# Another order of each engine's calls within a step of the attention stage

## The chip, the cores and the metric

The kernel runs on one core of a Trainium2 chip. The metric is the device time of one execution in microseconds; the figure compared is the median over several runs. A separate execution is recorded by the profiler and gives the trace.

## The reference, cut to what matters

The kernel computes a block of three parts over an input of 2 sequences x 4096 tokens x 256 features: a routed feed-forward part (8 experts, each token goes to its best two), a linear-attention part, and a second routed feed-forward part. The change touches only the attention part. Its core is a scan over chunks of 64 tokens, per sequence and head:

```python
def step(S, ch):
    Q, K, V, bt = ch
    Kb = K * bt
    Vb = V * bt
    A = jnp.eye(C) + jnp.tril(jnp.einsum('bhcd,bhed->bhce', Kb, K), -1)
    T = solve_triangular(A, I, lower=True)
    W = T @ Kb
    U = T @ Vb
    St = S.swapaxes(-1, -2)
    mid = U - W @ St
    O = Q @ St + jnp.einsum('bhcd,bhed->bhce', Q, K) * M @ mid
    S_new = S + mid.swapaxes(-1, -2) @ K
    return (S_new, O)
...
x = x + 0.5 * _L0_ffn_ref(_layernorm(x), ...)
x = x + _L0_attn_ref(_layernorm(x), ...)
x = x + 0.5 * _L0_ffn_ref(_layernorm(x), ...)
```

Q, K and V come from three projections, a causal convolution over 4 tokens and a silu; Q and K are normed. The output is normed per head, projected and added to x. The kernel also works out, while attention still runs, the gate of the second feed-forward part (which experts each finished token goes to) and scatters the finished rows into lists of rows per expert.

## The kernel before, in words

`build` runs three stages one after the other with a barrier between them: `ffn1`, `attention`, `ffn2`. In `attention` a tile is 128 tokens of each of the two sequences; there are NS = 32 tiles. `steps_of` unrolls the stage into 35 steps and a few more for the last gates. One step works on several tiles at once, like a pipeline: each engine's `body(f, g, t, s, u, v)` gets

- `f`: the tile whose norm, projections, convolution, silu and turning back run now (the front);
- `g`: the tile one behind, whose Gram products run and whose 16x16 diagonal blocks are inverted on GpSimd (`spread_blocks`, `take_blocks`, `invert_blocks`, `collect_inverses`; the blocks go through memory outside the core and back by small transfers on SyncE's queue, which end in the tiles `r16` and `i16`);
- `t`: two behind, whose inverse is grown from 16 to 32 to 64 (`first_products16`, which reads `r16` and `i16`, to `second_products64`);
- `s`: three behind, whose recurrent state, output and residual run (`state_in`, `out_in`, `mids`, `outputs`, `state_out`, `out_turn`, `out_project`, `residual`, `store_result`);
- `u`: four behind, whose gate products run;
- `v`: a batch of four finished tiles (with a position 0 to 3 in the cycle of four steps), whose routing runs (`load_batch`, `gate_norm`, `gate_first` in position 1, `gate_second`, `gate_exps`, `gate_sums` in position 2, `gate_scores`, `gate_ends`, `gate_places` and three `gate_scatter` calls in position 3, five more in position 0 of the next cycle).

The steps are called by their position 0, 1, 2, 3 in the cycle of four here. In the first three steps only `f`, then `g`, then `t` are there; in the last ones `f`, then `g`, then `t` are missing.

Nothing schedules the work at run time: every engine executes its calls in the order in which its `body` names them, and waits on semaphores where an operand or a buffer is not ready. The five `body` functions are the order written out by hand. SyncE executes no arithmetic; its `body` is the order in which the transfers of its queue are issued, and a wait there holds all transfers behind it. Among the functions that the change moves:

- `load_batch` (SyncE): reads a batch of four finished tiles back, two transfers of 512 KB, for the scatters.
- `load_weights` (SyncE): reads the expert weights of the second feed-forward part, in the step of the last tile.
- `column_sums` (TensorE) and `column_sums_out` (VectorE): sums over the gate's weights, once, in the first step that has a `t`.
- `clear_buffers` (VectorE): twelve memsets, once, in the step of the first tile.
- `x_low` (VectorE): the low part of the turned input, without which the projections `qkv` don't start. `history`: the three last tokens before the convolution.
- `remainder` (VectorE): V minus what the state gives, between `state_in` and `mids`. `residual` (VectorE): x plus the projected output; `out_in` of the next step waits for it, since it writes the same bank `ob`.
- `raw_out`, `tap0`, `silus`, `gate_turned` (ScalarE): copies of the projections, first tap of the convolution, silus, copy of the turned gate input.

## Time and profile before

| | |
|---|---|
| time, median of 3 runs | 1627.17 us (1624.81 to 1630.52) |
| time of the profiled execution | 1628.22 us |
| its span, first to last instruction | 1626.5 us |
| mean granted TensorE clock | 0.909 of full speed |
| attention stage in the span | about 397 to 1366 us |
| busy in the span: TensorE, VectorE, ScalarE, GpSimd | 83%, 76%, 54%, 61% |
| a step in the middle of attention | 26.3 to 28.4 us |

The profiled execution took 1.05 us more than the median of the three runs. 1.72 us of it lie outside the span. The rows further down have the start in us from the start of the span, the length in us, the engine, the line and operation, what is written from what, and the count; in brackets stands the idle time of the engine before it and the instruction whose end released it.

### The profile page before, as it was taken

To read this page: it belongs to the slowest core of one execution; us is meant where nothing else is said; L and a number is where in the kernel's file an instruction comes from. 1 tells how busy PE (TensorE), PEld (TensorE's weight loads), DVE (VectorE), ACT (ScalarE), POOL (GpSimd) and SP (SyncE) were. 2 spreads that over 40 slices of the span, in tenths; PEclk is the share of its full clock that TensorE was granted. 3 is DMA by queue.
4 is the path that set the end of the run, shared out by engine and by line. 5 is a ranking of instruction groups with operands and counts; after the bars stand their busy time and mean duration, and the time that the engine had idled before them with its cause. 6 is when DMAs were issued, how large, how long until landed. Compare 5 with 4: busy or idle time off the path is not lost. (4 is left out here: it accounts for less than half of the span.)

```text
span 1626.5 us, 36945 instructions
## 1 busy us (share of the span) xinstructions
PE 1344.8 (83%) x11688; PEld 1250.9 (77%) x11688; DVE 1237.7 (76%) x3235; ACT 875.4 (54%) x1725; POOL 986.1 (61%) x1719
## 2 busy tenths in 40 slices
PE   7673994994679999999999999899999761995996
PEld 7673994994568888888888888788888751995896
DVE  6664772673679999999999999899999645673574
ACT  2123772771356666657566666565666412772773
POOL 4762673575356566676675866766767622475366
PEclk8555997997699999999999999999999975998898
DMA  6426976671011213122213231222222245885782
GB/s 208 154 102 173 311 257 226 224 251 61 10 30 38 57 37 78 38 76 62 68 40 77 63 75 39 75 65 61 53 73 61 68 120 149 260 273 185 250 273 95
DMA packets 224026, 195.90 MB, mean 120 GB/s; under 512 B 105556, under 2 KB 186714, under 8 KB 223840
## 3 DMA queue, kind: packets, MB, share of 16 engines
q1 hardware_dynamic: 190560, 117.21, 26.4%
q0 software_dynamic: 24576, 67.94, 11.5%
q10 hardware_dynamic: 8704, 8.39, 1.8%
q8 instruction: 102, 1.67, 0.5%
q14 instruction: 84, 0.69, 0.1%
HBM read 103.68 MB, written 96.10 MB: 123 GB/s over the span
## 5 line engine op out<-in xcount | busy, mean ns | idle before, releaser
L1563 DVE SCALAR_TENSOR_TENSOR raw_w<-attn_raw,taps,raw_w 128x256 f32<-128x256 f32 x576 | 252.0, 495 | 17.9 <-ACT raw_w L1971 16.3
L468 PE MATMUL ffn_both<-ws,ffn_xhi 128*128 x1152 | 203.9, 289 | 0.6 <-issue 0.2
L2225 POOL TENSOR_TENSOR attn_inv<-attn_inv,attn_term 64x14 f32<-64x14 f32 (+6 forms) x448 | 147.8, 330 | 35.1
L468 PEld LDWEIGHTS ffn_both<-ws,ffn_xhi 128*128 128x128 f32 x1152 | 164.3, 192 | 3.0 <-issue 3.0
L2222 POOL TENSOR_TENSOR attn_term<-attn_small,attn_inv 64x14 f32<-64x14 f32 (+6 forms) x448 | 139.0, 310 | 35.1
L457 PE MATMUL ffn_both<-ident,ffn_xb 128*128 128x128 f32 x576 | 82.0, 290 | 93.7 <-ACT ffn_xb L752 93.7
L1202 PE MATMUL attn_fr<-attn_xhi,wqkv 128*128 128x256 f32 x768 | 148.7, 296 | 8.4 <-ACT attn_bth L1978 6.8
L457 PEld LDWEIGHTS ffn_both<-ident,ffn_xb 128*128 128x128 f32 x576 | 70.1, 150 | 95.9 <-ACT ffn_xb L752 74.9
L491 PE MATMUL ffn_yb<-ws,ffn_hhi 128*128 x576 | 119.5, 292 | 6.2 <-DVE ffn_hlo L667 6.2
L1202 PEld LDWEIGHTS attn_fr<-attn_xhi,wqkv 128*128 128x128 f32 x768 | 113.6, 194 | 10.0 <-ACT attn_bth L1978 7.4
L662 DVE TENSOR_TENSOR ffn_hid<-ffn_both,ffn_sil 128x512 f32<-128x512 f32 x72 | 49.8, 692 | 88.2 <-ACT ffn_sil L764 88.2
L468 PE MATMUL ffn_both<-ws,ffn_xlo 128*128 x576 | 116.1, 283 | 0.0
L657 DVE TENSOR_TENSOR ffn_xlo<-ffn_both,ffn_xhi 128x1024 fp32r<-128x1024 f32 x72 | 87.8, 1219 | 36.9 <-ACT ffn_xhi L759 36.8
L829 POOL DMA_INDIRECT second_rows<-ffn_more_rows,ffn_to x64 | 63.1, 985 | 85.3 <-DVE ffn_to L652 69.3
L752 ACT ACTIVATE ffn_xb<-ffn_more_rows 128x256 f32<-128x256 f32 x120 | 62.1, 591 | 78.3 <-DMA ffn_more_rows<-first_rows 42.5
L491 PEld LDWEIGHTS ffn_yb<-ws,ffn_hhi 128*128 128x128 f32 x576 | 94.2, 191 | 7.2 <-issue 7.2
L1262 PE MATMUL attn_tp<-ws 64*128 64x256 f32 x512 | 74.3, 407 | 21.7 <-DVE attn_tc L1638 11.1
L759 ACT ACTIVATE ffn_xhi<-ffn_both 128x1024 fp32r<-128x1024 f32 x72 | 73.9, 1027 | 34.0 <-PE ffn_both L457 34.0
L764 ACT ACTIVATE ffn_sil<-ffn_both 128x512 f32<-128x512 f32 x72 | 43.0, 597 | 90.5 <-PE ffn_both L468 90.5
L818 POOL DMA_INDIRECT first_rows<-ffn_xb,ffn_slots x64 | 65.4, 1022 | 41.0 <-DVE ffn_xb L642 23.7
L468 PEld LDWEIGHTS ffn_both<-ws,ffn_xlo 128*128 128x128 f32 x576 | 90.1, 192 | 0.0
L2145 POOL TENSOR_SCALAR attn_var_eps<-attn_mv 128x2 f32<-128x2 f32 x32 | 10.0, 312 | 131.5 <-DVE attn_mv L1528 131.3
(309 smaller groups left out, 4192.6 us busy)
## 6 DMA issues: line engine op xcount, KB each, us to landing
ffn_more_rows<-second_rows SPq DMA_DIRECT2D x56, 259.0 KB
ffn_xb<-second_rows SPq DMA_DIRECT2D x48, 259.0 KB
raw_w<-second_rows SPq DMA_DIRECT2D x40, 259.0 KB
ffn_more_rows<-first_rows SPq DMA_DIRECT2D x64, 131.0 KB
ffn_xb<-in_L_attn_x_dram SPq DMA_DIRECT2D x8, 1024.0 KB, 6.0
attn_xin<-x_after_first ACTq DMA_DIRECT2D x32, 256.0 KB, 2.8
attn_xres<-x_after_first SPq DMA_DIRECT2D x32, 256.0 KB, 2.8
x_after_attention<-attn_xres SPq DMA_DIRECT2D x32, 256.0 KB, 2.2
```

The lines of the kernel that those rows point to most:

```text
L457: last = pe.transpose(tr[:, q, j * P:(j + 1) * P], xs[:, k % 2, j, q * P:(q + 1) * P], ident[:])
L468: last = pe.matmul(hp[:, j, :], (xhi, xlo)[b][:, k % 2, q, j * P:(j + 1) * P], ws[:, bass.ds(experts[j], 1), a, q].rearrange("p o d -> p ( ...
L491: last = pe.matmul(yb[:, j, :], (hhi, hlo)[b][:, k % 2, j * P:(j + 1) * P], ws[:, bass.ds(experts[j], 1), a, 2].rearrange("p o d -> p (o d)"),
L657: dve.tensor_tensor(xlo[:, k % 2], tr, xhi[:, k % 2].bitcast(F32), ALU.subtract).then_inc(xlo_ready, 1)
L759: act.activation(xhi[:, k % 2], tr, ACT.Copy).then_inc(xhi_ready, 1)
L818: pool.indirect_dma_start(out=rows1, out_offset=bass.IndirectOffsetOnAxis(ap=slots[:, m % 2, j:j + 1], axis=0), in_=xb[:, m % 4, j, :], in ...
L829: pool.indirect_dma_start(out=rows2 if k < NSP else sums, out_offset=bass.IndirectOffsetOnAxis(ap=to[:, k % NW, j:j + 1], axis=0), in_=xw[ ...
L1202: last = pe.matmul(out, w[:, a, q, col], (xhi, xlo)[b][:, q, :], skip_group_check=True, start=(start and k == 0 and q == 0), stop=(k == 2 ...
L1262: last = pe.matmul(tp[:, h, s * 2 * P:(s + 1) * 2 * P], kq[a, par, q, s, 0, :], kq[a, par, q, s], start=(s == 0), stop=True, skip_group_ch ...
L1563: dve.scalar_tensor_tensor(acc[:, j, r], raw[:, j, r, :, tap:tap + P], taps[:, j, r, tap:tap + 1], acc[:, j, r], ALU.mult, ALU.add)\
L2222: pool.tensor_tensor(term[:, 0:k, 0:j], n[:, j + 1:, j:j + 1].broadcast_to([BP, k, j]), v[:, j:j + 1, 0:j].broadcast_to([BP, k, j]), ALU.m ...
L2225: pool.tensor_tensor(v[:, j + 1:, 0:j], v[:, j + 1:, 0:j], term[:, 0:k, 0:j], ALU.subtract)\
```

## The change

Within a step the calls stand in another order on SyncE, TensorE, VectorE and ScalarE. No operation, wait or buffer is added or removed. On GpSimd two calls change places that are never in the same step (positions 1 and 0), so its instructions stay as they are.

```diff
@@ -1164,16 +1164,16 @@
                     spread_blocks(g)
                 if s:
                     load_residual(s)
-                if s and isinstance(s[0], int) and s[0] == NS - 1:
-                    load_weights()
+                if v and v[1] == 1:
+                    load_batch(v)
                 if g:
                     take_blocks(g)
                 if s:
                     store_result(s)
-                if v and v[1] == 1:
-                    load_batch(v)
                 if g:
                     collect_inverses(g)
+                if s and isinstance(s[0], int) and s[0] == NS - 1:
+                    load_weights()
 
             sp.dma_start(gws[:], fresh.gate_w.rearrange("(c p) e -> p c e", p=P)).then_inc(g_loaded, 16)
             steps_of(sp, body)
@@ -1461,12 +1461,11 @@
                         pe.wait_ge(masks, 1)
                         pe.wait_ge(zeroed, 1 + ZEROED)
                     gram(g, 0)
-                if s:
-                    state_in(s, v)
                 if f:
                     x_turn(f)
                 if s:
                     out_in(s)
+                    state_in(s, v)
                 if g:
                     gram(g, 1)
                 if s:
@@ -1475,14 +1474,14 @@
                     qkv(f, 0)
                 if s:
                     outputs(s)
+                if t and isinstance(t[0], int) and t[0] == 0:
+                    column_sums()
                 if t:
                     first_products16(t)
+                if s:
+                    state_out(s)
                 if f:
                     qkv(f, 1)
-                if t and isinstance(t[0], int) and t[0] == 0:
-                    column_sums()
-                if s:
-                    state_out(s)
                 if t:
                     second_products16(t)
                 if f:
@@ -1858,20 +1857,23 @@
                         dve.wait_ge(masks, 1)
                     gram_out(g, 0)
                 if f:
-                    x_low(f)
-                    history(f)
                     if isinstance(f[0], int) and f[0] == 0:
                         clear_buffers()
                 if s:
                     remainder(s)
+                if f:
+                    x_low(f)
+                    history(f)
+                if v and v[1] == 2:
+                    gate_second(v)
                 if g:
                     gram_out(g, 1)
-                if t and isinstance(t[0], int) and t[0] == 0:
-                    column_sums_out()
                 if v and v[1] == 3:
                     gate_scores(v)
                 if v and v[1] == 2:
-                    gate_second(v)
+                    gate_sums(v)
+                if t and isinstance(t[0], int) and t[0] == 0:
+                    column_sums_out()
                 if v and v[1] == 1:
                     gate_norm(v)
                 if u:
@@ -1915,8 +1917,6 @@
                     scale_inverse(t)
                 if v and v[1] == 3:
                     gate_ends(v)
-                if s:
-                    residual(s)
                 if f:
                     betas(f)
                 if u:
@@ -1925,8 +1925,8 @@
                     gate_places(v)
                 if t:
                     second_out64(t)
-                if v and v[1] == 2:
-                    gate_sums(v)
+                if s:
+                    residual(s)
                 if f:
                     norms(f)
 
@@ -2078,10 +2078,10 @@
                 more = f and not (isinstance(f[0], int) and f[0] + 1 >= NS)
                 if f:
                     x_high(f)
+                if more:
+                    load_x(after(f))
                 if t:
                     side_by_side(t)
-                if more:
-                    load_x(after(f))
                 if s:
                     mid_out(s)
                 if f:
@@ -2094,8 +2094,8 @@
                 if v and v[1] == 2:
                     gate_exps(v)
                 if f:
+                    raw_out(f, 1)
                     silus(f, 0)
-                    raw_out(f, 1)
                     beta_tanh(f)
                     tap0(f, 1)
                 if t:
@@ -2105,10 +2105,11 @@
                     out_high(s)
                 if f:
                     raw_out(f, 2)
+                if u:
+                    gate_turned(u)
+                if f:
                     tap0(f, 2)
                     silus(f, 1)
-                if u:
-                    gate_turned(u)
                 if t:
                     first_out64(t)
                 if f:
```

Three places follow, as the instructions stand in the program.

**SyncE's transfers in the step where the inverse of the last tile is asked for** (position 1, last cycle). `attn_small` is the read of the diagonal blocks for GpSimd (`take_blocks`), `attn_xg` the read of a finished batch (`load_batch`), `small_inverses` what `collect_inverses` writes, `attn_r` and `attn_i` the tiles r16 and i16. Before:

```order
L1137 DMA small_blocks<-raw_w 16x8x16 x8
L1109 DMA attn_xres<-x_after_first 128x2x256
L1144 DMA attn_small<-small_blocks 64x256
L1114 DMA x_after_attention<-attn_xres 128x2x256
L1121 DMA attn_xg<-x_after_attention 128x4x256 x2
L1151 DMA small_inverses<-attn_inv 64x256
L1153 DMA small_inverses_turned<-attn_inv 64x16x16
L1157 DMA attn_r<-small_inverses_turned 128x1x128
```

Now:

```order
L1137 DMA small_blocks<-raw_w 16x8x16 x8
L1109 DMA attn_xres<-x_after_first 128x2x256
L1121 DMA attn_xg<-x_after_attention 128x4x256 x2
L1144 DMA attn_small<-small_blocks 64x256
L1114 DMA x_after_attention<-attn_xres 128x2x256
L1151 DMA small_inverses<-attn_inv 64x256
L1153 DMA small_inverses_turned<-attn_inv 64x16x16
L1157 DMA attn_r<-small_inverses_turned 128x1x128
```

The two big reads moved from behind the store of a tile (and ahead of the writes of the inverses) to ahead of the small read that GpSimd's inversion waits for. The same stands in every step of position 1 from the second cycle on, seven times in all.

**VectorE at the end of a step of position 3**: `attn_row` and `ends` are `gate_ends`, `attn_chosen` to `attn_xg` are `gate_places`, `attn_tc` from `attn_tp` is `second_out64`, `attn_xres` is `residual`, `attn_ss` begins `norms`. Before:

```order
L1649 TENSOR_TENSOR attn_tc<-raw_w,attn_cc 128x512 x2
L1819 TENSOR_TENSOR attn_row<-attn_sc,ends 128x128
L1822 TENSOR_TENSOR ends<-ends,attn_sc 128x16
L1699 TENSOR_TENSOR attn_xres<-attn_ob,attn_xres 128x512
L1572 TENSOR_SCALAR attn_beta<-attn_fr 128x8
L1716 COPY attn_glg<-attn_sc 128x16
L1828 TENSOR_TENSOR attn_chosen<-attn_picked,attn_row 128x128
L1830 TENSOR_REDUCE attn_slot<-attn_chosen 128x16
L1833 CAST attn_slots<-attn_slot 128x8
L1834 COPY attn_xg<-attn_slot 128x8
L1638 SCALAR_TENSOR_TENSOR attn_tc<-attn_tp,attn_cc 64x4x64 x2
L1580 TENSOR_REDUCE attn_ss<-raw_w 128x16
```

Now (the file's lines behind TensorE's `body` are one lower):

```order
L1648 TENSOR_TENSOR attn_tc<-raw_w,attn_cc 128x512 x2
L1818 TENSOR_TENSOR attn_row<-attn_sc,ends 128x128
L1821 TENSOR_TENSOR ends<-ends,attn_sc 128x16
L1571 TENSOR_SCALAR attn_beta<-attn_fr 128x8
L1715 COPY attn_glg<-attn_sc 128x16
L1827 TENSOR_TENSOR attn_chosen<-attn_picked,attn_row 128x128
L1829 TENSOR_REDUCE attn_slot<-attn_chosen 128x16
L1832 CAST attn_slots<-attn_slot 128x8
L1833 COPY attn_xg<-attn_slot 128x8
L1637 SCALAR_TENSOR_TENSOR attn_tc<-attn_tp,attn_cc 64x4x64 x2
L1698 TENSOR_TENSOR attn_xres<-attn_ob,attn_xres 128x512
L1579 TENSOR_REDUCE attn_ss<-raw_w 128x16
```

`residual` moved behind everything that it stood ahead of, up to `norms`; all these come earlier by its length. So it is at the end of every step that has an `s`.

**TensorE in the first step with a `t`**: `attn_sc` from `attn_gws` is `column_sums`, `attn_tp` from `attn_r` is `first_products16`, the rows at L1202 around it are the projections `qkv`, and `attn_tp` from `attn_x` is `second_products16`. Before:

```order
L1273 MATMUL attn_tp<-attn_r,attn_n 128x128 x4
L1202 MATMUL attn_fr<-attn_xhi,wqkv 128x256 x2
L1202 MATMUL attn_fr<-attn_xlo,wqkv 128x256 x2
L1202 MATMUL attn_fr<-attn_xhi,wqkv 128x256 x4
L1202 MATMUL attn_fr<-attn_xlo,wqkv 128x256 x2
L1202 MATMUL attn_fr<-attn_xhi,wqkv 128x256 x2
L1337 MATMUL attn_sc<-attn_gws,attn_ones 128x8 x2
L1281 MATMUL attn_tp<-attn_x,attn_i 128x128 x4
```

Now:

```order
L1337 MATMUL attn_sc<-attn_gws,attn_ones 128x8 x2
L1273 MATMUL attn_tp<-attn_r,attn_n 128x128 x4
L1202 MATMUL attn_fr<-attn_xhi,wqkv 128x256 x2
L1202 MATMUL attn_fr<-attn_xlo,wqkv 128x256 x2
L1202 MATMUL attn_fr<-attn_xhi,wqkv 128x256 x4
L1202 MATMUL attn_fr<-attn_xlo,wqkv 128x256 x2
L1202 MATMUL attn_fr<-attn_xhi,wqkv 128x256 x2
L1281 MATMUL attn_tp<-attn_x,attn_i 128x128 x4
```

`column_sums`, whose result VectorE copies out early in its own step, moved from behind the products with r16 and the second projection to ahead of both.

## Rows read from the trace of the kernel before

**Rows 1.** Busy time of each engine in 100 us of steady attention, granted clock, transfers:

```profile
core 0: us, PE busy (x) PEld busy (x) DVE busy (x) ACT busy (x) POOL busy (x), PEclk, DMA share, GB/s
1000.00:1100.00 100.00, 92.65 (x902) 83.85 (x900) 94.03 (x257) 62.40 (x135) 71.69 (x152) 1.00 0.24 61
```

**Rows 2.** Timeline of VectorE and TensorE in a step of position 0:

```profile
693.49 0.42 DVE L1599 TENSOR_TENSOR ws<-attn_tp,attn_upto 128x256 f32<-128x256 f32 x1
...
694.07 1.14 PE L1262 MATMUL attn_tp<-ws 64*128 64x256 f32 x8
...
699.82 0.89 DVE L1563 SCALAR_TENSOR_TENSOR raw_w<-attn_raw,taps,raw_w 128x256 f32<-128x256 f32 x2 [0.91 <-ACT raw_w L1971]
...
706.83 0.69 DVE L1682 TENSOR_TENSOR attn_on<-attn_ob,attn_og 128x512 f32<-128x512 f32 x1 [0.76 <-POOL attn_og L2255]
```

**Rows 3.** Timeline of GpSimd at the end of the step before:

```profile
689.08 0.60 POOL L2230 COPY attn_inv<-attn_inv 64x256 f32<-64x256 f32 x1
690.09 1.13 POOL L2164 DMA_INDIRECT first_rows<-attn_xg,attn_slots  x1 [0.41 <-DVE attn_xg L1834]
```

**Rows 4.** Timeline: SyncE's inverses after a batch read, TensorE's use, SyncE's one step on:

```profile
636.84 0.62 SPq L1153 DMA_DIRECT2D small_inverses_turned<-attn_inv  x1
642.28 0.63 SPq L1157 DMA_DIRECT2D attn_r<-small_inverses_turned  x1
...
645.40 1.06 PE L1273 MATMUL attn_tp<-attn_r,attn_n 128*128 128x128 f32 x8
...
664.29 0.62 SPq L1153 DMA_DIRECT2D small_inverses_turned<-attn_inv  x1
666.90 0.63 SPq L1157 DMA_DIRECT2D attn_r<-small_inverses_turned  x1
```

**Rows 5.** Timeline of the last tile's inverse: SyncE, GpSimd, SyncE, TensorE:

```profile
1279.09 0.48 SPq L1144 DMA_DIRECT2D attn_small<-small_blocks  x1
...
1281.41 0.72 POOL L2218 TENSOR_TENSOR attn_inv<-attn_eye,attn_small 64x256 f32<-64x256 f32 x1 [0.78 <-DMA attn_small<-small_blocks]
...
1296.25 0.63 SPq L1157 DMA_DIRECT2D attn_r<-small_inverses_turned  x1
...
1299.20 2.07 PE L1273 MATMUL attn_tp<-attn_r,attn_n 128*128 128x128 f32 x8 [6.17 <-DMA attn_i<-small_inverses]
```

**Rows 6.** Timeline around the last tile's state and the last scatters:

```profile
1309.70 0.69 DVE L1699 TENSOR_TENSOR attn_xres<-attn_ob,attn_xres 128x512 f32<-128x512 f32 x1
...
1311.42 0.75 DVE L1638 SCALAR_TENSOR_TENSOR attn_tc<-attn_tp,attn_cc 64x256 f32<-64x256 f32 x2 [0.52 <-PE attn_tp L1329]
...
1313.40 2.05 PE L1411 MATMUL attn_sc<-ws,attn_tc 128*128 128x128 f32 x16
...
1332.20 1.11 POOL L2164 DMA_INDIRECT first_rows<-attn_xg,attn_slots  x1 [10.95 <-DVE attn_xg L1834]
```

**Rows 7.** The weights: last issue, its transfer (issue to landing), first use on VectorE:

```profile
1316.77 2.81 SPq L198 DMA_DIRECT2D raw_w<-in_L_ffn_w_dram  x1
...
raw_w<-in_L_ffn_w_dram SPq DMA_DIRECT2D x1, 1024.0 KB, 9.4
...
1359.07 7.03 DVE L1941 TENSOR_TENSOR ws<-raw_w,ws 128x768 fp32r<-128x768 f32 x8
```

**Rows 8.** Timeline of the first tile's step, VectorE and ScalarE:

```profile
404.96 0.69 DVE L1543 TENSOR_TENSOR attn_xlo<-attn_fr,attn_xhi 128x512 fp32r<-128x512 f32 x1 [0.27 <-ACT attn_xhi L1956]
...
409.37 0.91 ACT L1971 ACTIVATE raw_w<-attn_raw,taps 128x256 f32<-128x256 f32 x2
...
411.07 0.69 DVE L1525 BATCH_NORM_STATS2 attn_stats<-attn_xin 128x6 f32<-128x256 f32 x2
...
411.96 2.43 DVE L1563 SCALAR_TENSOR_TENSOR raw_w<-attn_raw,taps,raw_w 128x256 f32<-128x256 f32 x6
```

**Rows 9.** Timeline of the first step with a `t`, TensorE and VectorE:

```profile
457.58 1.16 PE L1273 MATMUL attn_tp<-attn_r,attn_n 128*128 128x128 f32 x8 [3.44 <-DMA attn_i<-small_inverses]
...
460.54 0.17 DVE L1838 COPY attn_colsum<-attn_sc 128x8 f32<-128x8 f32 x1 [6.17 <-PE attn_sc L1337]
...
467.15 1.86 DVE L1563 SCALAR_TENSOR_TENSOR raw_w<-attn_raw,taps,raw_w 128x256 f32<-128x256 f32 x4 [0.92 <-ACT raw_w L1971]
```

4 lines of the change are left out of this document (2 added, 2 removed).

## The prediction, written before the result was known

> **What bounds the kernel now.** I began with the busy time per stretch. In the middle of attention VectorE is busy for 94.03 of 100 us and TensorE for 92.65 at full clock [rows 1]; part of VectorE's other 6 us is the gap between instructions, so I went through its timeline for the places where a wait is named. The waits recur by position. Position 0 waits 0.91 us for the first tap, and at most cycles 0.76 us more for GpSimd's factor `og` [rows 2]; four early steps without gate work have the first of these as well. Position 3 has a shorter one, and positions 1 and 2 have none. So VectorE is the bound of attention, and what a reordering can win there is what VectorE waits, not what other engines wait. Next come the two ends, where the pipeline fills and drains: there an engine's wait is time on the path at once. The longest two: VectorE's 6.17 us for `column_sums` [rows 9], and TensorE's 6.17 us for the last tile's r16 and i16 [rows 5].
>
> **The middle, the loop behind the first tap.** The wait of 0.91 us closes a loop: VectorE's `gram_out` ends at 693.91, TensorE starts the second Gram product 0.16 us behind it at 694.07, and `mids`, the first projection, `raw_out` and `tap0` follow without a hole until VectorE's first tap at 699.82 [rows 2]. The change puts `x_low` and `history` behind `remainder`, `state_in` behind `x_turn` and `out_in`, and `second_out64` ahead of `residual`. All of these act before the second Gram product or beside the loop; its start is set by `gram_out`, which keeps its place, and its members keep theirs. I take 0. `state_out` ahead of the second projection, `raw_out` ahead of the first silu, `gate_turned` ahead of the third tap: VectorE waits for none of them in the middle, 0.
>
> **The middle, GpSimd in position 0.** `residual` is now behind `gate_places`, so the slots are ready 0.6 us earlier (its length is 0.69 us [rows 6], and neighbours overlap by nearly 0.1). GpSimd's last copy of the inversion ends at 689.68, and the first scatter starts at 690.09 after a wait of 0.41 us for the slots [rows 3]. The wait goes, the chain of eight scatters, `values` and `out_factor` comes 0.4 us earlier, and so does `og`, for which VectorE waits 0.76 us [rows 2]. Five cycles look like this: 5 x 0.4 = 2.0 us less. Bounds: 0, if something else on GpSimd is late, and 5 x 0.6 = 3 us.
>
> **The middle, the batch read in position 1.** In the trace the read of a batch (1 MB) stands ahead of the writes of the inverses. It costs them: from the issue of the second write to the issue of the next read, which waits for it, 5.44 us pass, against 2.61 us one step on where nothing is in front [rows 4]. So 1 MB in front costs a small transfer of SyncE's queue 2.8 us, and 2.0 to 2.4 in the cycles behind. Now the read stands in front of `take_blocks` instead. GpSimd's inversion starts later by that and by the issue, about 3 us, but the inverses then go out with nothing in front, which gives 2.2 to 2.8 us back. r16 and i16 land 0.5 to 1 us later than now. TensorE needs them at 645.40, 3.12 us after the issue at 642.28 [rows 4]; where it did wait for them, 2.95 us passed [rows 5], so its slack is some 0.2 us. VectorE has more: in position 2 `gate_sums`, three small instructions, now comes before it reads the product. I take 0.15 us for each of six cycles, +1 us; bounds 0 and 1 us each, +6.
>
> **The drain, the last inverse.** In the last cycle there is nothing to hide this. GpSimd starts the last inversion at 1281.41, having waited 0.78 us for the small read issued at 1279.09, and TensorE waits 6.17 us for what comes of it [rows 5]; the whole end of the stage hangs on that. The old batch read was issued long before the inverses were ready, so here nothing is given back. The small read is issued 0.5 us later (two issues of 0.5 us, of which 0.6 fall into a gap) and has 1 MB in front for 2.0 to 2.8 us. I take 0.5 + 2.5 = +3.0 us. Bounds: 0.5, if transfers of one queue don't hold each other up that soon after issue, and 4.4. The Trainium skill (DMA: Bandwidth & Descriptors, Queues, rings and completion order) says that SyncE's transfers share one ring on each DMA engine, whose descriptors are taken in order; the stretched inverses agree. Its Bandwidth section gives 6.15 us for 1 MB; as an estimate by that page the small read would land at about 1284.7, so the loss would be 3.3 us and the sum 0.3 us higher.
>
> **The drain, the last tile's state.** `out_in` waits for `residual` of the tile before, and is now ahead of `state_in`. In the step of the last tile nothing of `g` or `f` stands before them on TensorE. `residual` ran at 1309.70; now it follows `second_out64`, which waits for TensorE and ends at 1312.17 [rows 6]. So it ends at 1312.8, `out_in` and `state_in` take 2 us, the first `remainder` 0.4, and `mids` starts at about 1315.0 instead of 1313.40 [rows 6]: +1.6 us. In the other drain steps the wait for r16 hides it. At the very end `gate_places` is ahead of `residual`, so the scatters that begin at 1332.20 [rows 6] begin 0.6 us earlier: -0.6. Together +1.0; bounds -0.6 and +2.
>
> **The drain, the weights.** The last of them was issued at 1316.77 and landed 9.4 us later, at 1326 [rows 7]. Behind the store of the last tile, which is written just before the scatters begin at 1332.20 [rows 6], all moves by some 20 us, to about 1346. VectorE's first use is at 1359.07 [rows 7], and ScalarE needs under 1 us for the piece ahead of it. The cover is 12 us: 0. If the weights slow the scatters beside them, that is late next, up to +1.5.
>
> **The fill, the first tile.** `clear_buffers` took VectorE until 411.07, from `x_low`'s end at 405.65 with `history` between, 5.3 us, while the first projection ran [rows 8]. It is now ahead of `x_low`: `x_low` starts some 5.1 us later (it waited 0.27), the projections with it. The first tap was done at 409.8 and used at 411.96, so 2.1 us were slack [rows 8]: +3.0. `raw_out` of the second projection is now ahead of the first silu, a copy of 0.5 us less before the last projection: +2.6. Everything in the fill, GpSimd's inversions too, moves with it. Bounds +1.5 and +5.1.
>
> **The fill, column_sums.** VectorE waits 6.17 us until 460.54 for it, and only then norms the next input and runs the taps, up to the wait that ends at 467.15 [rows 9]. With `column_sums` directly behind the first projection, all of that lies in the wait for r16, which TensorE gets at 457.58 [rows 9]. Then the chain is: products with r16 until 458.7, their mask on VectorE until 459.4, four taps until 461.0, silu 0.6, `beta_rows` on TensorE until 462.2, `beta_tanh` and first tap until 463.0. VectorE's second convolution starts at 463.0 instead of 467.15: -4.1. Bounds -2.5 (if r16 of the next tile becomes late, whose inversion on GpSimd doesn't move) and -6.
>
> **Sum.** -2.0 + 1.0 + 3.0 + 1.0 + 0 + 2.6 - 4.1 = +1.5 us, so 1628.22 + 1.5 = 1629.7 for an execution like the profiled one. That one took 1.05 us more than the median of the runs; against the median the sum is 1627.17 + 1.5 = 1628.7. I say 1629.
>
> **The rivals.** *(A) Late r16 takes hold in the middle.* In position 2 ScalarE must now copy the second projection between two loads of its function table, and TensorE runs `state_out` before that projection; if r16 is 1 us late, all of that is, and VectorE waits. From a delay of about 0.7 us on it costs what exceeds that. If nothing is given back the delay is 2.8 us [rows 4], which costs 2.1 us a cycle: six cycles make 12.6 instead of 1, so 1627.2 + 1.5 + 11.6 = 1640; half as bad, 1634. For it: the slack of 0.2 us. Against it: the inverses are relieved.
> *(B) The loop does shorten.* If what stood between `gram_out` and the first tap held it up in a way the timeline doesn't name, the 0.91 us [rows 2] shrink in some eleven steps: -0.5 x 11 = -5.5, and with the fill's gain at its bound of -6, 1627.2 + 1.5 - 5.5 - 1.9 = 1621. Against it: TensorE starts 0.16 us behind `gram_out`.
> *(C) Small transfers aren't held up.* If the small read slips past the 1 MB, the drain costs 0.5 and the middle nothing: 1.5 - 2.5 - 1 = -2.0, 1625. Against it: [rows 4].
> *(D) Nothing to be seen.* All terms are small and cancel, 1627.
>
> **How the numbers follow.** Chances: my sum with its neighbours, (C) and (D) within 0.3% (4.9 us, about what a measurement of this kernel can tell from none) 0.57; slower than that, by (A) or by the drain and the fill at their upper bounds, 0.27; faster, by (B) or a longer gain in the fill, 0.16. The range reaches from (B) at 1621, less 1 for what it leaves open, to halfway between (A) at its half and at its whole, 1637.
>
> **What would show it.** In the changed profile: the first scatter of a batch without its wait and `og`'s wait at about 0.35 us; the inverses' next issue 3 us behind instead of 5.4; the last inversion starting some 3 us later relative to its step; the wait for `column_sums` gone and a longer one before the first tap of the first tile; the first-tap wait in position 0 still 0.9 us. I am wrong if positions 1 and 2 show new waits of VectorE for r16's products or a tap, or if steps are shorter than 26.3 us.

## The result and the profile after

The changed kernel takes 1637.66 us, median of six runs; the kernel before took 1630.34 beside it. The ratio is 1.0051, with a 95% interval of 1.0028 to 1.0074: slower by 7.3 us by the medians, by 8.3 by the ratio. The profiled execution took 1637.81 us, of which 1636.1 are span. In the rows of the code after, the lines of VectorE are one lower than before, those of GpSimd one higher, those of TensorE and ScalarE the same.

Four instants on VectorE cut the span: the first `norm_stats`, the third `norms`, the last `norms`, and the first cast in the second expert stage, which waits for gathered rows. Here they are in the timeline of the kernel before, then of the changed one.

```profile
400.04 0.75 DVE L1525 BATCH_NORM_STATS2 attn_stats<-attn_xin 128x6 f32<-128x256 f32 x2 [15.93 <-DMA attn_xin<-x_after_first]
...
477.29 1.22 DVE L1580 TENSOR_REDUCE attn_ss<-raw_w 128x16 f32<-128x1024 f32 x1 [0.77 <-ACT raw_w L1993]
...
1267.26 1.22 DVE L1580 TENSOR_REDUCE attn_ss<-raw_w 128x16 f32<-128x1024 f32 x1
...
1373.65 0.17 DVE L652 CAST ffn_to<-ffn_more_rows 128x4 int32<-128x4 f32 x1 [7.55 <-DMA ffn_more_rows<-first_rows]
```

```profile
397.70 0.75 DVE L1524 BATCH_NORM_STATS2 attn_stats<-attn_xin 128x6 f32<-128x256 f32 x2 [15.20 <-DMA attn_xin<-x_after_first]
...
474.88 1.22 DVE L1579 TENSOR_REDUCE attn_ss<-raw_w 128x16 f32<-128x1024 f32 x1 [1.53 <-ACT raw_w L1993]
...
1268.66 1.22 DVE L1579 TENSOR_REDUCE attn_ss<-raw_w 128x16 f32<-128x1024 f32 x1
...
1383.80 0.17 DVE L652 CAST ffn_to<-ffn_more_rows 128x4 int32<-128x4 f32 x1 [11.03 <-DMA ffn_more_rows<-first_rows]
```

The stage ahead of attention, which the change doesn't touch, was 2.34 us shorter in this execution, and what follows the cast 0.6 us shorter. The fill took 77.18 us instead of 77.25, the middle 793.78 instead of 789.97, the drain 115.14 instead of 106.39: -0.1, +3.8 and +8.75. My sum had -1.5, -1.0 and +4.0. By positions, the middle's +3.8 are +1.8 us in position 0, -1.2 in position 1, +3.5 in position 2, -0.6 in position 3 and +0.3 in the first steps.

**Middle, position 2.** The timeline of a step that begins at 633.37 (the one of [rows 4]): SyncE, TensorE, ScalarE, VectorE.

```profile
633.37 0.36 SPq L1114 DMA_DIRECT2D x_after_attention<-attn_xres  x1
...
637.91 0.62 SPq L1153 DMA_DIRECT2D small_inverses_turned<-attn_inv  x1
642.05 0.63 SPq L1157 DMA_DIRECT2D attn_r<-small_inverses_turned  x1
...
644.69 1.16 PE L1273 MATMUL attn_tp<-attn_r,attn_n 128*128 128x128 f32 x8 [1.27 <-DMA attn_i<-small_inverses]
...
648.20 0.60 ACT L1962 ACTIVATE attn_raw<-attn_fr 128x512 f32<-128x512 f32 x1 [1.56 <-PE attn_fr L1202]
...
651.44 1.68 DVE L1562 SCALAR_TENSOR_TENSOR raw_w<-attn_raw,taps,raw_w 128x256 f32<-128x256 f32 x4 [0.55 <-ACT raw_w L1971]
```

The reader sees a chain: the read of r16 is issued 8.68 us into the step instead of 6.76, TensorE waits 1.27 us for it, the second projection and its copy come late, and VectorE waits 0.55 us for a tap. This is the chain of rival (A). The step took 28.16 us instead of 27.11. The other half us is an instruction that waits for nothing by name and is stretched, beside GpSimd's `values`:

```profile
639.07 1.04 POOL L2240 TENSOR_TENSOR ws<-attn_vtok,attn_kn 128x512 f32<-128x512 f32 x1
...
639.48 0.71 DVE L1775 TENSOR_TENSOR attn_picked<-attn_ranked,attn_rank 128x64 f32<-128x64 f32 x1
```

It took 0.22 to 0.23 us in all six steps of the kernel before, where `values` ran 3.0 us into the step and met other instructions. Behind the late inversion `values` runs at 5.7 and meets this one in all six: 0.71 to 0.74 us. It takes two moves for that: `gate_second`, to which the instruction belongs, now stands further ahead and runs it at 6.1 us of the step instead of 7.9. In e4 below `values` runs late (4.7 to 5.7) and `gate_second` where it was, in e3 it is the other way round (3.0), and in both the instruction takes 0.22 to 0.23.

**Middle, position 0.** GpSimd's end of the inversion and first scatter, then VectorE's waits for the first tap and for `og`, two cycles apart.

```profile
688.22 0.61 POOL L2231 COPY attn_inv<-attn_inv 64x256 f32<-64x256 f32 x1
689.03 1.13 POOL L2165 DMA_INDIRECT first_rows<-attn_xg,attn_slots  x1 [0.20 <-issue]
...
698.65 0.88 DVE L1562 SCALAR_TENSOR_TENSOR raw_w<-attn_raw,taps,raw_w 128x256 f32<-128x256 f32 x2 [0.94 <-ACT raw_w L1971]
...
705.65 0.69 DVE L1681 TENSOR_TENSOR attn_on<-attn_ob,attn_og 128x512 f32<-128x512 f32 x1 [0.75 <-POOL attn_og L2256]
...
926.93 0.69 DVE L1681 TENSOR_TENSOR attn_on<-attn_ob,attn_og 128x512 f32<-128x512 f32 x1 [1.84 <-POOL attn_og L2256]
```

The scatter no longer waits for the slots [rows 3], but the copy ahead of it ends 0.38 us before the step's `norms` (689.21) instead of 0.69 us before them (690.37), so `og` isn't earlier. The waits for it in the six cycles are 0.75, 0.75, 1.84, 1.84, 1.84 and 0.36 us, in the kernel before 0.76, 0.76, 0.76, 2.16, 0.76 and 0.35: 1.8 us more in sum, as much as position 0 became longer. The loop behind the first tap is as it was.

**Drain.** The last inverse (SyncE, GpSimd, TensorE), to hold against [rows 5]:

```profile
1281.25 0.49 SPq L1144 DMA_DIRECT2D attn_small<-small_blocks  x1
...
1286.18 1.26 POOL L2219 TENSOR_TENSOR attn_inv<-attn_eye,attn_small 64x256 f32<-64x256 f32 x1 [4.53 <-DMA attn_small<-small_blocks]
...
1303.59 2.08 PE L1273 MATMUL attn_tp<-attn_r,attn_n 128*128 128x128 f32 x8 [7.61 <-DMA attn_i<-small_inverses]
```

From issue to use 4.93 us pass, with the megabyte ahead, instead of 2.32. The last tile's state, against [rows 6]:

```profile
1317.28 0.67 DVE L1698 TENSOR_TENSOR attn_xres<-attn_ob,attn_xres 128x512 f32<-128x512 f32 x1
...
1318.01 1.57 PE L1400 MATMUL attn_ob<-attn_state,ws 128*128 128x128 f32 x8 [1.52 <-DVE attn_xres L1698]
...
1319.37 1.92 PE L1390 MATMUL attn_sc<-attn_state,ws 128*128 128x128 f32 x8
1320.47 0.42 DVE L1657 TENSOR_TENSOR ws<-ws,attn_sc 128x256 f32<-128x256 f32 x1 [2.52 <-PE attn_sc L1390]
...
1321.08 2.42 PE L1411 MATMUL attn_sc<-ws,attn_tc 128*128 128x128 f32 x16
...
1338.92 1.11 POOL L2165 DMA_INDIRECT first_rows<-attn_xg,attn_slots  x1 [9.62 <-DVE attn_xg L1833]
```

`out_in` waits for `residual`, `state_in` stands behind it, `mids` behind both: the mechanism that I priced, with a clock that I didn't. By windows, the stretch about the state in the kernel before and in the changed one:

```profile
core 0: us, PE busy (x), PEclk, DMA share, GB/s
1311.40:1315.50 4.10, 3.98 (x34) 1.00 0.83 232
```

```profile
1316.60:1323.00 6.40, 4.99 (x30) 0.73 0.27 84
```

And the end of attention: the last batch read of the kernel before, then of the changed one the weights' last issue and transfer, the last batch read, and the scatter that waits for it.

```profile
1343.70 0.92 SPq L1121 DMA_DIRECT2D attn_xg<-x_after_attention  x2
```

```profile
1344.82 2.42 SPq L198 DMA_DIRECT2D raw_w<-in_L_ffn_w_dram  x1
...
raw_w<-in_L_ffn_w_dram SPq DMA_DIRECT2D x1, 1024.0 KB, 10.5
...
1353.82 0.92 SPq L1121 DMA_DIRECT2D attn_xg<-x_after_attention  x2
...
1360.15 1.10 POOL L2165 DMA_INDIRECT first_rows<-attn_xg,attn_slots  x1 [9.22 <-DMA attn_xg<-x_after_attention]
```

The weights now move under the scatters of the batch before. The read waits for those to land: it is issued 10.1 us later than before, while the slots of the last batch are only 6.7 us later (VectorE writes the last `attn_xg` at 1358.29, before at 1351.55). Slots no longer end last here; the megabyte does. The last eight scatters themselves also take longer, from the first at 1360.15 to the eighth 11.1 us instead of 9.2 (first at 1352.01). The eighth, before and now:

```profile
1361.16 1.43 POOL L2164 DMA_INDIRECT first_rows<-attn_xg,attn_slots  x1 [0.30 <-issue]
```

```profile
1371.30 1.43 POOL L2165 DMA_INDIRECT first_rows<-attn_xg,attn_slots  x1 [0.30 <-issue]
```

**Fill.** VectorE in the first tile's step and in the first step with a `t`, against [rows 8, 9]:

```profile
407.80 0.63 DVE L1542 TENSOR_TENSOR attn_xlo<-attn_fr,attn_xhi 128x512 fp32r<-128x512 f32 x1
...
412.69 1.68 DVE L1562 SCALAR_TENSOR_TENSOR raw_w<-attn_raw,taps,raw_w 128x256 f32<-128x256 f32 x4 [3.22 <-ACT raw_w L1971]
...
452.93 0.17 DVE L1837 COPY attn_colsum<-attn_sc 128x8 f32<-128x8 f32 x1 [0.16 <-PE attn_sc L1337]
...
458.54 0.69 DVE L1605 TENSOR_TENSOR attn_x<-attn_tp,attn_same 128x512 f32<-128x512 f32 x1 [3.73 <-PE attn_tp L1273]
...
462.43 0.35 DVE L1611 SCALAR_TENSOR_TENSOR attn_r<-attn_r,attn_odd_even,attn_tp 128x128 f32<-128x128 f32 x1 [1.62 <-PE attn_tp L1281]
```

The wait for `column_sums` has turned into waits for products with r16 and i16.

### The profile page after: what moved, and what is told of

It reads as the page before. It is cut to its first block and busy times, and to the rows that moved or that the text cites. A ratio compares the mean times of both kernels' runs of the same rounds, so it can differ in the third digit from the quotient of the medians.

```text
span 1636.1 us, 36944 instructions
## 1 busy us (share of the span) xinstructions
PE 1344.9 (82%) x11688; PEld 1254.8 (77%) x11688; DVE 1238.1 (76%) x3235; ACT 878.5 (54%) x1725; POOL 985.3 (60%) x1719
## 5 line engine op out<-in xcount | busy, mean ns | idle before, releaser
L1202 PE MATMUL attn_fr<-attn_xhi,wqkv 128*128 128x256 f32 x768 | 148.2, 295 | 10.6 <-DVE attn_xlo L1542 6.7
L1202 PEld LDWEIGHTS attn_fr<-attn_xhi,wqkv 128*128 128x128 f32 x768 | 113.2, 194 | 12.2 <-issue 7.7
L1962 ACT ACTIVATE attn_raw<-attn_fr 128x512 f32<-128x512 f32 x96 | 57.5, 599 | 119.8 <-PE attn_fr L1202 119.4
L2165 POOL DMA_INDIRECT first_rows<-attn_xg,attn_slots x64 | 66.5, 1040 | 36.1 <-issue 17.3
```

Of the source, the lines that this page charges most:

```text
L1202: last = pe.matmul(out, w[:, a, q, col], (xhi, xlo)[b][:, q, :], skip_group_check=True, start=(start and k == 0 and q == 0), stop=(k == 2 ...
L2165: pool.indirect_dma_start(out=rows1, out_offset=bass.IndirectOffsetOnAxis(ap=slots[:, j:j + 1], axis=0), in_=xg[:, j, :], in_offset=None). ...
```

## The experiments

Eighteen more runs were made, in five sets, each set beside the kernel before on its own chip. On the chips of sets 1 and 4 the kernel before took 1628.5 and 1629.2 us. On those of sets 2, 3 and 5 it took 1756 to 1768: an execution of it there (below, e9) reached the first `norm_stats` at 461.81 us and spent 315.7 us behind the first cast, against 400.04 and 252.9. I compare only ratios, and stage times of chips of one kind. All stage times together; "middle" is from the third `norms` to the last, "pos. 2" the sum of its six steps of position 2 between cycles' ends, "drain" from the last `norms` to the first cast:

```
kernel                          fill  middle  pos. 2   drain  ratio to before, 95%
chips where before takes 1628 to 1630 us
before                         77.25  789.97  163.95  106.39
changed                        77.18  793.78  167.49  115.14  1.0051 (1.0028-1.0074)
e15 changed, again             76.85  792.87  167.55  113.56  1.0055 (1.0040-1.0069)
e1  batch read back            77.21  795.35  167.15  111.67  1.0036 (1.0023-1.0049)
e2  weights back               77.24  790.36  166.55  112.82  1.0011 (0.9998-1.0025)
e3  both back                  79.38  794.38  166.26  109.39  1.0025 (1.0007-1.0043)
e4  before + batch read early  77.18  792.95  166.92  109.70  1.0042 (1.0025-1.0059)
e13 residual back              79.48  794.42  166.86  110.29  1.0045 (1.0030-1.0060)
e14 clear_buffers back         74.63  794.43  167.41  114.15  1.0051 (1.0038-1.0064)
e16 the version of e7          75.68  790.66  165.03  105.43  0.9974 (0.9958-0.9990)
chips where before takes 1756 to 1768 us
e9  before, again              80.83  799.45  164.55  105.65
e5  e3 + residual back         77.76  798.90  164.17  106.34  0.9964 (0.9941-0.9987)
e6  before + residual late     78.85  804.12  166.08  107.16  1.0015 (0.9987-1.0043)
e17 the same, again            81.99  805.00  167.40  108.03  1.0020 (0.9995-1.0045)
e7  e5 + state, clear back     74.27  797.22  164.22  105.25  0.9945 (0.9923-0.9967)
e10 the same, again            75.59  801.26  163.75  105.43  0.9964 (0.9940-0.9989)
e8  before + sums early        75.59  799.21  163.95  105.98  0.9972 (0.9947-0.9997)
e18 the same, again            75.59  798.92  165.20  105.99  0.9978 (0.9954-1.0003)
e11 changed, batch on ScalarE  76.87  805.61  165.15  112.78  1.0021 (0.9997-1.0045)
e12 e7, batch on ScalarE       74.29  805.54  166.40  108.35  0.9989 (0.9964-1.0013)
```

How far one profile repeats is seen from equal kernels: position 2 within 1.3 us, the drain within 1.6, the whole middle only within some 4 (e7 and e10, which ran on two chips). So I read differences of position 2 above 2 us and of the drain above 1.6, and of the middle none alone. The times have intervals of 2 to 4 us each way. Two more things move without a cause in the edits. The fill is 76.9 to 77.2 us in four kernels with the changed order there and 79.4 to 79.5 in two others with the same order (e3, e13), so it repeats only within 2.6 us. And the stage ahead of attention, which no edit touches, ends (by the first `norm_stats`) between 393.62 us (e2) and 400.04 (the kernel before) in the profiled executions on chips of the first kind; so a time and the sum of the stage times here can differ by several us.

**Set 1: SyncE's order.** Theory 1 was that SyncE's two moves cost nearly all. e1 puts the batch read back, e2 the weights, e3 both; e4 makes the first move alone in the kernel before.

```diff
 SyncE's body, from the changed kernel to e3:
-                if v and v[1] == 1:
-                    load_batch(v)
+                if s and isinstance(s[0], int) and s[0] == NS - 1:
+                    load_weights()
                 if g:
                     take_blocks(g)
                 if s:
                     store_result(s)
+                if v and v[1] == 1:
+                    load_batch(v)
                 if g:
                     collect_inverses(g)
-                if s and isinstance(s[0], int) and s[0] == NS - 1:
-                    load_weights()
```

> The changed kernel with one edit undone: SyncE issues the batch read behind the result's store again. Theory 1 (the batch read ahead of the small read holds up SyncE's chain of blocks, inversion, inverses): the middle of attention (norms of the third tile to norms of the last) was 793.78 us in the changed kernel and 789.97 before, so it gives back 2 to 4 us there; and the last inversion's wait for its blocks falls from 4.5 to about 0.8 us, 3 us more. Sum 5 to 7 us less than the changed kernel, so at most 3 us more than the kernel before. Rival (the new orders of TensorE, ScalarE and VectorE cause the middle's loss): the middle stays at 793 to 794, only 3 us come back, 5 us more than before.

> The changed kernel with one edit undone: SyncE issues the weights' loads ahead of the last tile's small reads again. Theory 1 (the weights' traffic slows the scatters ahead of the last batch's read, which then comes late): the last batch's read is issued about 2.5 us behind the eighth scatter instead of 5.9, VectorE's slots are the last thing that the last eight scatters wait for, and from the last slots to the first gathered row it is 3 to 3.5 us shorter; 3.5 us less than the changed kernel, 4.5 more than before. Rival (the last batch's scatters are slow by themselves): no change against the changed kernel, 8 us more than before.

> The changed kernel with SyncE's order wholly as before; the orders of the other four engines stay changed. Theory 1: the sum of the two edits undone apart, 9 to 10 us less than the changed kernel, so 1 to 2 us less than the kernel before; what is left is the last tile's state (+3), the first tile (+1.4), and the sums of columns (-1.5 to -4), and the middle within 1 us of 789.97. Rival (compute engines' orders cost the middle): 3 to 4 us more than before.

> The kernel before with one edit alone: the batch read ahead of the small read. Theory 1: the loss is SyncE's, so the middle is 2 to 4 us longer than before, with a wait of VectorE for a tap or for the products in position 2, and the last inversion starts 3 us late: 5 to 7 us more than before. Rival (the batch read only costs where ScalarE copies the second projection behind the late inverses): the middle stays within 1 us of 789.97, only the 3 us of the last inversion show.

The drain came out near what was expected and adds up: the batch read costs 3.3 us there (e4 against before), 3.5 and 3.4 (changed against e1, e2 against e3; e15 against e1 only 1.9). Read at the inversion itself it is plainer: on chips of the first kind the last one starts 17.3 to 17.8 us behind the last `norms` in all six kernels with the early read, and 14.1 to 14.3 in the four without. The weights cost 2.3 (e1 against e3), 0.7 to 2.3 against the changed kernel's two executions. In e4's timeline a small read in position 1 with the megabyte right ahead of it takes 5.04 us from issue to use:

```profile
617.66 1.02 SPq L1121 DMA_DIRECT2D attn_xg<-x_after_attention  x2
618.78 0.48 SPq L1144 DMA_DIRECT2D attn_small<-small_blocks  x1
...
623.82 1.02 POOL L2218 TENSOR_TENSOR attn_inv<-attn_eye,attn_small 64x256 f32<-64x256 f32 x1 [2.77 <-DMA attn_small<-small_blocks]
```

In the middle theory 1 failed by half, and in e1 and e3 the rivals came: by their ratios e1 took 5.9 us and e3 4.1 us more than before, where theory 1 had at most 3 more and 1 to 2 less; e4 took 6.8 more, as expected. e4 does make position 2 3.0 us longer, with VectorE waiting for the products with r16 in four of the six steps, 0.2 to 0.4 us in three and 1.62 in one; but with SyncE's order wholly back (e3) position 2 is still 2.3 us longer than before, and the time is not below it. e2's time, 1.8 us above before, is lower than theory 1 allows, and e3 isn't below e2, as it should be by 3.4 us of drain; e3's fill was 2.1 us longer, which no edit of it explains. In e2's profiled execution the stage ahead of attention was 6.4 us shorter than in the kernel before; whether that holds for its other executions no profile shows. Something else delays r16. In e3 SyncE stores the result 0.01 to 0.11 us behind the `norms`, in the kernel before 0.8 to 1.8 us ahead of the next ones (means by position): `store_result` waits for `residual`, and the writes and reads of the inverses stand behind it in SyncE's program.

**Set 2: the residual.** e5 is e3 with `residual` back; e6 moves it alone in the kernel before; e7 puts back `state_in` and `clear_buffers` too; e8 is the kernel before with `column_sums` early alone.

```diff
 VectorE's body, from e3 to e5:
+                if s:
+                    residual(s)
                 if f:
                     betas(f)
...
                 if t:
                     second_out64(t)
-                if s:
-                    residual(s)
                 if f:
                     norms(f)
 TensorE's body, from e5 to e7:
+                if s:
+                    state_in(s, v)
                 if f:
                     x_turn(f)
                 if s:
                     out_in(s)
-                    state_in(s, v)
 VectorE's body, from e5 to e7:
-                if f:
-                    if isinstance(f[0], int) and f[0] == 0:
-                        clear_buffers()
                 if s:
                     remainder(s)
                 if f:
                     x_low(f)
                     history(f)
+                    if isinstance(f[0], int) and f[0] == 0:
+                        clear_buffers()
 TensorE's body, from before to e8:
+                if t and isinstance(t[0], int) and t[0] == 0:
+                    column_sums()
                 if t:
                     first_products16(t)
                 if f:
                     qkv(f, 1)
-                if t and isinstance(t[0], int) and t[0] == 0:
-                    column_sums()
```

> The changed kernel with SyncE's order as before and, besides, VectorE's residual back ahead of betas. The two runs that undid SyncE's batch read left the middle at 794 to 795 us, so theory 1 fell for the middle. Theory 2: the late residual holds up SyncE's store of the result (issued 0.05 us behind the norms instead of 0.3 to 0.8 ahead of them, and in front of the inverses), so the reads of r16 and i16 are issued at 7.76 instead of 6.54 us of the step in position 2, at 5.69 instead of 4.64 in position 3, at 5.43 instead of 3.52 in position 0. With the residual back these return to within 0.3 us of the kernel before, the waits of VectorE for the tap in position 2 go, and the middle falls from 794.4 to 790 or 791; the last tile's step, in which out_in waits for the residual, becomes 1 to 2 us shorter too (109.4 us from the last norms to the first gathered rows, to 107.5 or 108). Sum: 4 to 6 us less than with SyncE alone as before, so 0 to 2 us less than the kernel before. Rival (ScalarE's and TensorE's new orders around the second projection cost the middle): the reads move, but the middle stays at 793 or more and the waits for the tap stay.

> The kernel before with one edit alone: residual behind gate_sums and second_out64, directly ahead of the norms. Theory 2: the store is issued behind the norms, the reads of r16 and i16 are 1 to 1.9 us later in the step than before, the middle is 2 to 4 us longer than 789.97, the drain up to 1 us longer: 2 to 5 us more than before. Rival (only ScalarE's and TensorE's orders make a late r16 count): reads late, middle within 1 us of before, time within 1 us of before.

> The changed kernel with SyncE's order, the residual, state_in and clear_buffers all back where they were; what stays changed are column_sums early, gate_sums, x_low and history behind remainder, state_out and raw_out ahead, and GpSimd. Theory 2 and the stage times: middle 790 or 791, from the last norms to the first gathered rows 106.4 as before, the first tile as before (26.2 us from its statistics to its norms), the next two tiles 1.5 us shorter through column_sums: 1 to 2 us less than the kernel before. Rival (other orders cost as well): 2 us or more above the kernel before, with the loss in the middle.

> The kernel before with one edit alone: TensorE's column_sums directly behind the first projection, ahead of the products with r16. VectorE's wait of 6.17 us for it falls to under 0.3; by the changed kernel's trace (49.59 us from the first norms to the third instead of 51.06) that gives back 1.5 us; by my prediction's sum it would be 4.1. Everything else within 0.5 us of before. So 1.5 us less than before if the trace of the changed kernel is right, 4 if the new first tile there hid part of the gain.

With the residual back, position 2 is 164.17; moved alone, 166.08 against 163.95 of e8 beside it: 2.1 us, of which one wait of 1.15 us for r16's products in one step is half. The drain is 106.34 us after e3's 109.39 (on the other kind of chip, where the kernel before's is 0.7 shorter). Against the expectations e5, e7 and e8 were faster than the theory had them, by their ratios 6.3, 9.7 and 4.9 us below before instead of 0 to 2, 1 to 2 and 1.5 to 4; e6 was 2.6 above, within an interval that holds 0. SyncE's timeline in position 2, first e6 (residual late, step begins at 699.55), then e16 (residual in its place, step begins at 631.69):

```profile
699.56 0.38 SPq L1114 DMA_DIRECT2D x_after_attention<-attn_xres  x1
699.99 1.06 SPq L1121 DMA_DIRECT2D attn_xg<-x_after_attention  x2
...
701.67 0.62 SPq L1153 DMA_DIRECT2D small_inverses_turned<-attn_inv  x1
706.71 0.63 SPq L1157 DMA_DIRECT2D attn_r<-small_inverses_turned  x1
```

```profile
630.89 0.38 SPq L1114 DMA_DIRECT2D x_after_attention<-attn_xres  x1
...
633.01 0.62 SPq L1153 DMA_DIRECT2D small_inverses_turned<-attn_inv  x1
638.04 0.63 SPq L1157 DMA_DIRECT2D attn_r<-small_inverses_turned  x1
```

From the second write to the read it is 5.04 and 5.03 us; the whole train starts 0.8 us later in the step. In positions 3 and 0, where nothing else is in front, the late store's own transfer is: the mean time of the read of r16 in the step goes from 4.22 to 5.66 us (e8, e6) and from 3.30 to 4.60 (position 0 without its last cycle).

**Set 3: which queue, and how well it repeats.** e9 is the kernel before, e10 is e7. e11 and e12 are the changed kernel and e7 with the batch read taken out of SyncE's body and issued by ScalarE behind `first_rows`:

```diff
+            def load_batch(v):
+                n = v[0]
+                wait(act, stored, 64 * (n + 1))
+                wait(act, gscattered, 16 * GB * n)
+                for s in range(2):
+                    act.dma_start(xg[:, s:GB:2, 0:DM], x2_v[n, s]).then_inc(xg_loaded, 16)
 ScalarE's body:
                 if t:
                     first_rows(t)
+                if v and v[1] == 1:
+                    load_batch(v)
```

> The kernel before, unchanged, once more with a profile: how far its stage times repeat. Theories 1 and 2 read causes from the sums over six steps by position; if they are right to read them, position 2 repeats at 163.95 within 0.5 us, position 0 at 163.8 within 1.5, the time from the last norms to the first gathered rows at 106.4 within 0.5. If these scatter by 2 us or more, what I read from them is noise.

> The version with SyncE's order, the residual, state_in and clear_buffers back, once more, since the chip of its first run took 1756 us for the kernel before instead of 1628. By its stage times there (fill 3.0 us shorter than before, drain 1.1 shorter, position 2 equal) it is 3 to 5 us faster than before here too. Rival: a part of the 9 us that it won there belongs to that chip's slow transfers (position 0 took 172.7 us instead of 175.3), and without them only the 1.7 us of the column sums are left, within 0.3% of before.

> The changed kernel with one edit: the batch read is issued on ScalarE's queue, behind first_rows in position 1, less than 1 us from the time at which SyncE issued it; the same megabyte moves at the same time, but not in front of SyncE's small transfers. If the order in SyncE's queue is what held up the small read, the inversion of position 1 starts at 15 us of the step as before the change instead of 18.2, the last one 14.2 us behind the last norms instead of 17.5; position 2 stays above 163.95 (the residual is still late) by about 2 us; drain 3.4 us shorter than 115.1; together 3 to 4 us less than the changed kernel, so 4 to 5 more than before. Rival (the megabyte takes the transfer engines' time whatever queue it is in): the inversion starts at 17 us or later, no gain.

> The version with the three edits back, and the batch read on ScalarE's queue. If the queue's order is what holds, the writes of the inverses in position 2 have nothing in front either, the reads of r16 and i16 are issued at 4.7 us of the step as in position 3 instead of 6.5, and the slack in position 2 grows; VectorE, which bounds that step, doesn't profit at once: position 2 at 163.5 to 164, the rest as in the version it is made from, within 1 us of it. Rival (bandwidth, not order): the reads stay at 6 us or later, and the last inversion starts later than 14.2 us.

e9 missed what it expected: it ran on the slower kind of chip, where position 0 took 174.7 us instead of 163.8 and the fill 80.83; position 2 came within 0.6 and the drain within 0.8 instead of 0.5. From this and the other pairs I took the bounds above. e10 repeated e7's gain within its interval, but on the slower kind of chip again, so its rival stayed open until e16. In e11 the inversion of position 1 starts 17.2 us into the step (mean of six), against 15.05 before and 18.17 in the changed kernel; the last one 16.6 us behind the last `norms`, against 14.15 and 17.52. Of the 3.1 to 3.4 us about 2.2 to 2.5 stay though SyncE's queue has no megabyte in front. The rows (ScalarE's queue, SyncE, GpSimd; step begins at 671.87):

```profile
681.94 0.93 ACTq L2078 DMA_DIRECT2D attn_xg<-x_after_attention  x2
...
685.94 0.49 SPq L1144 DMA_DIRECT2D attn_small<-small_blocks  x1
...
688.31 0.73 POOL L2226 TENSOR_TENSOR attn_inv<-attn_eye,attn_small 64x256 f32<-64x256 f32 x1 [1.87 <-DMA attn_small<-small_blocks]
```

The small read itself is quick now, 2.37 us; but SyncE issues it 14.1 us into the step instead of 12.7, for it waits for the blocks. ScalarE issues the megabyte 10.1 us into the step, 1.7 us earlier than SyncE did, so it goes out beside the eight writes of the blocks, and they land later. So taking it out of SyncE's queue did free the small read behind it, and moved most of the cost to the small writes beside it. Whether a megabyte issued on ScalarE's queue behind the blocks would cost anything is not tested. The Trainium skill (DMA: Bandwidth & Descriptors, Queues, rings and completion order) says beside its rule of one ring in order that each DMA engine takes turns between the queues that have work, a packet at a time; this case doesn't contradict it: the writes in SyncE's queue landed later beside a megabyte in ScalarE's. No run here shows the turns themselves. e12 shows the same in the good version, as its rival had it: position 2 2.2 to 2.7 us longer than e7 and e10, the drain 3.

**Set 4: what was open.** e13 and e14 undo one edit each in the changed kernel (`residual`, `clear_buffers`; diffs as above), e15 is the changed kernel, e16 is e7.

> The changed kernel with one edit undone: residual back ahead of betas; SyncE's order stays changed. Theory 2 (late residual, late store, late inverses; and out_in of the last tile, which is now ahead of state_in, waits for it): from the last norms to the first gathered rows 112 us instead of 115.1, position 2 at 166.5 to 167 (the batch read alone keeps it there), the reads of r16 in positions 3 and 0 at 4.6 and 3.5 us; 3 to 5 us less than the changed kernel. Rival (the drain's loss is out_in's new place by itself): the drain stays at 115.

> The changed kernel with one edit undone: clear_buffers back behind history. From the first statistics to the first norms 24.7 us, as in the version with three edits back, instead of 27.6; all else as in the changed kernel; 3 us less than the changed kernel. Rival (x_low and history behind remainder, or the second copy's new place, cost the first tile): it stays at 26 to 27.6 and the time does too.

> The changed kernel, unchanged, once more: 0.5% above the kernel before within 0.25% on either kind of chip if its loss is in the middle's position 2, the drain and the fill, whose stage times repeat (115.1 us drain, 167.5 position 2, 27.6 first tile). Rival: on a chip with slower transfers part of the loss vanishes behind the scatters of position 0, ratio 1.002 or less.

> The version with SyncE's order, the residual, state_in and clear_buffers back, for the third time. It was 0.55% and 0.36% faster than before on two chips with slow transfers. By stage times alone: fill 1.7 to 3 us shorter, drain 0.5 to 1 shorter, position 2 equal: ratio 0.997 to 0.998; if the gain needs slow transfers, 0.999 to 1.

The loss repeats: 1.0055. e13's drain is 3.3 to 4.9 us shorter than the changed kernel's, so the loss about the last tile's state belongs to `residual`: the two orders of `out_in` and `state_in` differ by 1 us at most where the residual is early (e5 106.34; e7 and e10 105.25 and 105.43). From the end of the last inversion to `mids` it is 22.8 to 23.4 us in the six kernels on these chips with the late residual and `out_in` ahead, with a granted clock of 0.73 about the state, and 20.3 to 20.7 in the four others, with 1.00. With the late residual but `state_in` ahead (e6, e17) it is 21.4 and 22.5, beside 20.9 to 21.2 (e8, e9, e18), at 1.00. So the whole loss takes both moves. e13's ratio fell by only 0.001, 1.6 us where 3 to 5 were expected, though; its fill was 2.6 us longer (79.48), as e3's. In both the granted clock over the first 28 us is 0.56 instead of 0.62 as in the changed kernel; but it is 0.56 in the kernel before too, so what makes these two fills long is open. e14's fill is 2.2 us shorter (74.63 against 76.85), its first tile 1.9 (25.69 against 27.56), where 2.9 were expected; the 2.2 are less than the 2.6 by which equal fills differ, and the time shows less than 1 us of it, within its interval. e16 is faster than the kernel before here too.

**Set 5.** e6 and e8 once more.

> The kernel before with the late residual alone, once more; its first run fell on a chip of 1756 us, where position 0 hides much. Theory 2: reads of r16 issued 1 us later in positions 2 and 3 than in the kernel before, position 2 at 166 instead of 163.95, drain about 107.2; 2 to 4 us more than before (ratio 1.0015 to 1.0025). Rival (VectorE makes it up in the next step): position 2 is longer but positions 1 or 3 are shorter by the same, ratio within 0.001 of 1.

> The kernel before with the early column_sums alone, once more. 75.6 us from the first statistics to the third norms instead of 77.25; the rest as before; ratio 0.999 if its worth is the 1.7 us of the fill, 0.997 if, as on the other chip, more comes with it.

The late residual: position 2 2.2 us longer than in e18 beside it, drain 2.0 longer, ratio 1.0020 after 1.0015; both intervals just hold 1. Two waits for r16's products, of 1.20 and 0.71 us, are most of the 2.2. The early sums: 75.59 again; against e9's 80.83 that is 5.2 us on these chips, which fits the ratios 0.9972 and 0.9978 here. Alone they never ran on the other kind; against its 77.25 the same 75.59 would be 1.7 us, and e16, with more moves, has 75.68 there.

## Why the prediction was wrong, step by step

1629 was forecast, 1620 to 1637 the range, 1637.66 came. The direction had 0.27. What failed most is the drain, +8.75 us for a forecast of +4.0: the last tile's state was mis-sized, and the weights' move was put at nothing. Next is the middle, +3.8 for -1.0, where `residual`'s hold on SyncE's queue had no term and the gain on GpSimd didn't come, and then the fill, where `column_sums` gave 1.7 instead of 4.1.

- *The loop behind the first tap, 0.* Right: 0.94 us after, 0.91 before [rows 2].
- *GpSimd in position 0, -2.0.* Wrong. "The wait goes, the chain ... comes 0.4 us earlier" took the end of the inversion as fixed. It moved back with the late chain; `og` won nothing, and over the six cycles VectorE's waits for it grew by 1.8 us. Waits of 0.75 to 2.16 us occur in e1 and e3 as well, and one of 2.16 in the kernel before; which small delay decides it I didn't find.
- *The batch read in position 1, +1.* Wrong, and bounded rightly (+6): alone it made position 2 3.0 us longer (e4). One reading was off: against the step behind it, a megabyte in front cost the inverses 1.6 to 3.2 us in the cycles after the first, not 2.0 to 2.4. Two steps of the argument failed. The first is "the inverses then go out with nothing in front, which gives 2.2 to 2.8 us back". Alone (e4) it gives 1.5 to 1.9 back. In the changed kernel the write to read takes 4.1 and 4.4 us in the first two cycles [here 637.91 to 642.05] against 5.4 and 5.9: 1.3 and 1.5 back, r16 late by 1.9 and 1.7 us, and all of VectorE's waits, 1.3 us together; these two steps hold 2.4 of the 3.5 us. In the other four it takes 2.6 us, r16 is 0.7 to 1.0 us late as forecast, and VectorE doesn't wait. The second is that I priced only waits: in all six steps one instruction of `gate_second` is stretched by half a microsecond. In e15 that is so in three of the six, and in the other three the instruction two ahead of it is stretched instead, 0.95 us for 0.22. What the stretch costs isn't shown: the fifth and sixth step have it and are 0.1 and 0.0 us longer than before, since VectorE's taps took 0.3 to 0.5 us less there.
- *What had no term at all:* `residual` is what `store_result` waits for, and the inverses stand behind the store on SyncE. I named the slots and `out_in` as what the move touches, and not the queue. Worth 2.1 and 2.2 us in position 2 alone (e6, e17), just above what I can read, and not additive to the batch read, since both delay the same r16: together 3.5, and with the early read in place putting `residual` back gives 0.6 (e13).
- *The last inverse, +3.0.* Right: 3.4 at the start of the inversion, 3.3 to 3.5 in the drain (1.9 against e15). The mechanism was given as order within a queue; in e11 the small read behind the megabyte is freed, but about two thirds of the loss remain, since the writes ahead of it now meet the megabyte.
- *The last tile's state, +1.6, and the scatters, -0.6.* The mechanism was right, the first term is 3.1 (from the end of the last inversion to `mids`: 1293.09 to 1313.40 before, 1297.65 to 1321.08 after, 20.3 and 23.4), and the second is 0.55 (VectorE's `ends` row, ahead of `residual`'s old place, comes 7.27 later, the scatter 6.72). Mis-sized were the clock, 0.73 instead of 1.00 about `out_in` and `state_in` (after waits of 7.61 and 1.52 us TensorE spends part of that stretch at 1.2 instead of 2.4 GHz, and `out_in` takes 1.57 us where the same eight matmuls take 1.16 at full clock, as in e13 at 1319.80), and 0.6 us ahead of `residual`.
- *The weights, 0, up to +1.5.* They landed at 1355.3, not 1346, and ScalarE, which starts on them at 1346.93 in the kernel before, waited 1.6 us for them: the 12 us were counted to VectorE's use, and there was hardly any cover to ScalarE's. What failed besides is "that is late next": the scatters that they slow are what the last batch read waits for. 0.7 to 2.3 us of drain. From the first scatter of the batch before to the cast it is 43.0 to 44.9 us in the five kernels on these chips with late weights, against 41.3 to 41.6 in the five without: at least 1.4 us more. Of the changed kernel's 3.4 there, 1.4 are the late read and 2.0 the last eight scatters, which take 9.6 to 11.1 us in every kernel with late weights and 9.2 in every other; what slows them isn't shown, for by then the weights have landed.
- *The first tile, +2.6.* 1.4 (27.59 against 26.19 us from the first `norm_stats` to the first `norms`); `clear_buffers` alone is 1.9 (e14).
- *`column_sums`, -4.1.* The size failed. The chain was nearly right up to the products (their mask forecast to end at 59.4 us of the fill; e8: 59.95), but then i16's products, which the sum left out, made VectorE wait again, 1.1 to 1.6 us. In e8 the second convolution starts 2.9 us earlier (64.2 us of the fill, before 67.1), and by the third `norms` 1.7 are left (75.59 against 77.25, and 77.18 in e4). In the changed kernel TensorE's granted clock is 0.70 instead of 0.90 in the 17 us behind, that is longer at 1.2 GHz; what that costs isn't shown, for e8 and e16 have 0.85 and 0.72 there and fills equal to 0.1 us.

```profile
460.04:477.04 17.00, 10.88 (x115) 9.40 (x116) 14.41 (x35) 8.13 (x18) 11.56 (x32) 0.90 0.02 5
```

```profile
457.70:474.70 17.00, 14.41 (x124) 13.09 (x123) 12.11 (x28) 8.19 (x18) 9.44 (x28) 0.70 0.04 7
```

(The kernel before, then the changed one; the clock is the third value from the end.)

With the measured terms of its two profiled executions the sum is: fill -0.1 and -0.4, middle +3.8 and +2.9, drain +8.75 and +7.2: 12.5 and 9.7 us, where the ratios show 8.3 and 9.0. In the first the stages ahead and behind, which no edit touches, were 2.9 us shorter than in the kernel before, which gives the 9.6 us between the two profiled times; in the second they were 3.5 us shorter. The rivals: (A)'s chain is what happened in the first two cycles, far below its half: it had 12.6 us for position 2 and 6 at half, and 3.5 came, 1.3 of them waits. It had shared the 0.27 for slower with the drain and the fill, and it is the drain that made the kernel slower. The sentence "I am wrong if positions 1 and 2 show new waits of VectorE for r16's products or a tap" was fulfilled by three waits of 0.23 to 0.55 us in position 2, less than the cost.

The version without the batch read's, the weights', the residual's, `state_in`'s and `clear_buffers`' moves beats both kernels: 0.9974 on a chip like the first, 0.9945 and 0.9964 on the others. The early `column_sums` alone gave 0.9972 beside the 0.9945, about half; on the first kind of chip the fill holds 1.6 us of a gain of 4.2, and the drain 1.0.

## What to carry to other kernels

When a call moves, ask which queue waits for its semaphore, and what stands behind that wait: here a 0.7 us addition on the busiest engine, moved behind its neighbours, held up a store by 0.8 us and with it the next tile's inverse. A large transfer goes where no small transfer that the critical path waits for is in flight; changing its queue gave back about a third here. In this drain a wait cost twice, once itself and once in the clock that TensorE ran at behind it; and the last thing to land, not the last thing to be computed, decided where the weights could be read.

## What the runs showed of the hardware that wasn't expected

A VectorE `tensor_tensor` of 128x64 with both inputs in SBUF took 0.71 to 0.74 us instead of 0.22 to 0.23 when it began while GpSimd's 128x512 multiply was running, in all six steps, and ended 0.08 us behind it (640.19 and 640.11 in the rows above). In e15 another of this form took 0.95 us and ended 0.08 us behind it too. The page of the profile lists no wait for that: it is busy time. The Trainium skill (SBUF — State Buffer, Who interferes with whom) states the rule, that such an instruction contends with one of GpSimd that reads SBUF and that the second to start blocks until the first is through; the trace agrees with it. And the kernel before took 8% longer in three of the five sets: of 137 us (spans 1763.4 and 1626.5) some 124 lie outside attention's fill and middle, and the steps of positions 1 to 3 took the same time to 1%.
